# Gated state-space block and expert layer on one core: dt*u*B of two pairs by ScalarE's scaling and TensorE's transpose

## What is computed

```python
def step(state, xs):
    d_t, B_t, C_t, u_t = xs
    dA = jnp.exp(d_t[..., None] * A)
    state = state * dA + (d_t * u_t)[..., None] * B_t[:, None, :]
    y_t = jnp.einsum('ben,bn->be', state, C_t)
    return (state, y_t)
...
y = y + D[None, :, None] * u
y = y * jax.nn.silu(z)
```

## Time and profile before

| what | value |
|---|---|
| three runs | 563.35, 566.0 and 566.44 us; median 566.0 us |
| profiled execution | 564.01 us, of which the span is 562.3 us |
| mean granted clock of PE | 0.975 |
| PE busy | 503.3 us (90%), weight loads 379.6 us |
| POOL busy | 481.5 us (86%) |
| DVE busy | 459.7 us (82%) |
| ACT busy | 395.1 us (70%) |
| HBM | 66 GB/s over the span |

### The profile page before, as it was taken

The page is one execution under the profiler, slowest core; times in us unless marked ns, Lnnn a source line. Parts: engine busy times, 40 slices in busy tenths (PEclk is TensorE's granted clock), DMA queues, the critical chain, the costliest instruction groups (busy, mean ns, idle before and its releaser), DMA issues.

```text
span 562.3 us, 9366 instructions
## 1 busy us (share of the span) xinstructions
PE 503.3 (90%) x3146; PEld 379.6 (68%) x3146; DVE 459.7 (82%) x842; ACT 395.1 (70%) x702; POOL 481.5 (86%) x361
## 2 busy tenths in 40 slices
PE   6577988988789999999999999999999998999496
PEld 2156977868576878579786967686676676567452
DVE  2798999969899989688999989696877788787640
ACT  3468688577958686577958685688877886796321
POOL 0179999999999999989999999799999999888600
PEclk9978999999999999999999999999999999999869
DMA  5792000146120001063300000363000000000000
GB/s 113 289 354 89 2 2 1 38 134 208 75 76 2 1 0 57 27 256 136 106 8 19 2 20 2 142 213 138 1 20 19 20 2 19 20 21 0 20 0 37
DMA packets 18130, 37.82 MB, mean 67 GB/s; under 512 B 5521, under 2 KB 6033, under 8 KB 18082
## 3 DMA queue, kind: packets, MB, share of 16 engines
q1 hardware_dynamic: 18082, 37.22, 19.2%
HBM read 32.75 MB, written 4.46 MB: 66 GB/s over the span
## 4 chain that ended last, share of the span: by engine, by line
PE 52%; ACT 14%; POOL 13%; DVE 11%; issue 8%; DMA 1%; DVEq 0%; ACTq 0%; SPq 0%; POOLq 0%
PE p_s L700 14%; PE p_y L719 11%; POOL state L523 8%; PE p_v L751 6%; PE p_f L742 5%; DVE state L1144 4%; PE p_tr L666 4%; POOL dbu L510 3%; ACT da L923 3%; PE p_pr L629 2%; DVE x L1092 2%; ACT p_s L923 2%; PE p_pr L622 2%; ACT L875 2%; PE p_pr L641 2%
## 5 line engine op out<-in xcount | busy, mean ns | idle before, releaser
L523 POOL TENSOR_TENSOR state<-state,c_bc 128x1024 f32<-128x1024 f32 (+1 forms) x160 | 306.5, 1929 | 15.4 <-DVE state L1144 12.5
L1144 DVE TENSOR_TENSOR_SCAN state<-da,p_s 128x512 f32<-128x512 f32 (+1 forms) x158 | 172.7, 1103 | 27.9 <-PE p_s L700 26.2
L700 PEld LDWEIGHTS p_s<-pair_b,du_t 128*128 128x128 f32 x1264 | 162.3, 195 | 36.5 <-issue 23.5
L700 PE MATMUL p_s<-pair_b,du_t 128*128 128x128 f32 x1264 | 177.0, 280 | 4.3 <-DVE state L1144 3.2
L719 PE MATMUL p_y<-ident,state 128*128 128x128 f32 x1024 | 149.6, 274 | 1.2 <-POOL state L523 1.2
L923 ACT ACTIVATE da<-delta,a_neg 128x512 f32<-128x512 f32 (+1 forms) x190 | 119.2, 642 | 25.2 <-DVE state L1144 24.7
L719 PEld LDWEIGHTS p_y<-ident,state 128*128 128x128 f32 x1024 | 119.5, 141 | 21.8 <-issue 16.3
L510 POOL TENSOR_TENSOR dbu<-du,pair_b 128x1024 f32<-128x1024 f32 (+1 forms) x64 | 116.5, 1820 | 2.9 <-DMA pair_b<-bc_rows 2.9
L1144 DVE TENSOR_TENSOR_SCAN state<-p_s,dbu 128x512 f32<-128x512 f32 (+1 forms) x98 | 101.1, 1037 | 5.5 <-POOL dbu L510 4.4
L923 ACT ACTIVATE p_s<-delta,a_neg 128x512 f32<-128x512 f32 (+1 forms) x130 | 74.9, 581 | 38.6 <-DVE state L1144 37.9
L742 PE MATMUL p_f<-u_sb,h_t 128*128 128x512 f32 x112 | 55.2, 595 | 1.5 <-DVE gw L1236 1.5
(11 more groups left out here) (172 smaller groups left out, 616.4 us busy)
## 6 DMA issues: line engine op xcount, KB each, us to landing
c_bc<-bc_rows SPq DMA_DIRECT2D x32, 512.0 KB, 5.5
pair_b<-bc_rows SPq DMA_DIRECT2D x13, 512.0 KB, 5.6
xs<-in_x SPq DMA_DIRECT2D x16, 256.0 KB, 4.5
out<-ot SPq DMA_DIRECT2D x14, 256.0 KB, 2.0
cx<-in_ctx_t SPq DMA_DIRECT2D x4, 512.0 KB, 3.7
u_sb<-in_u_w SPq DMA_DIRECT2D x1, 1024.0 KB, 6.8
v_sb<-in_v_w SPq DMA_DIRECT2D x1, 1024.0 KB, 14.7
out<-state SPq DMA_DIRECT2D x2, 256.0 KB, 2.0
```

The source lines that it names most:

```text
L523: eng.tensor_tensor(pair, pair, c_bc[:, 2 * p:2 * p + 2, c0:c0 + w], ALU.mult).then_inc(po_cs, 1)
L700: mm = eng.matmul(p_s[g % BANKS][:, t * P:(t + 1) * P], du_t[:, f % 2, t, :], diagonals_of(n // 2)[:, n % 2, c0 // P + t, :], start=(t == ...
L1144: eng.tensor_tensor_scan(slot(g)[:, 0:w], decayed, added, first, ALU.mult, ALU.add).then_inc(ve_scan, 1)
```

## The change

In phases 3, 7 and 11 the tiles of the last two PE pairs (pairs 6 and 7 in phase 3, pairs 5 and 7 in phases 7 and 11) are made in another way. ACT scales each of the 4 blocks of `du_t` by the column of `b_t`, one instruction for each block, and writes the result over the diagonal of the same block in `pair_b`, which is not needed again. PE then only transposes the block, with the identity as the moving operand. It makes 12 tiles, 48 blocks, in this way. ACT's four scalings of a tile stand behind `decay` of n = 0, 2, 4 and 6 and wait for the copy of du and for PE's last use of the diagonal, in the phase before. `make_dbu` of such a tile waits for the last of its four scalings. `copy_b` waits for all scalings of the earlier batches, since it writes `b_t`.

```diff
+    def by_scale(f, p):
+        b, k = PHASE[f][:2]
+        return k == Q - 1 and b + 1 < B and p in pe_pairs(b)[-2:]
+
+    SCALED = [(f, n, t) for f in range(F) for n in range(NS) if by_scale(f, n // 2) for t in range(Q)]
...
-                if b == 0 and n == 0:
+                scaled = by_scale(f, n // 2)
+                if scaled:
+                    eng.wait_ge(ac_scale, SCALED.index((f, n, Q - 1)) + 1)
+                elif b == 0 and n == 0:
...
                 for t in range(w // P):
-                    mm = eng.matmul(p_s[g % BANKS][:, t * P:(t + 1) * P], du_t[:, f % 2, t, :], diagonals_of(n // 2)[:, n % 2, c0 // P + t, :],
-                                    start=(t == 0), stop=(t == w // P - 1))
+                    to = p_s[g % BANKS][:, t * P:(t + 1) * P]
+                    by_b = diagonals_of(n // 2)[:, n % 2, c0 // P + t, :]
+                    if scaled:
+                        mm = eng.matmul(to, by_b, ident[:, :], is_transpose=True, start=(t == 0), stop=(t == w // P - 1))
+                    else:
+                        mm = eng.matmul(to, du_t[:, f % 2, t, :], by_b, start=(t == 0), stop=(t == w // P - 1))
...
                     if b > 1:
                         eng.wait_ge(ac_diag, 2 * Q * (b - 1))
+                    eng.wait_ge(ac_scale, sum(PHASE[f][0] < b for f, n, t in SCALED))
...
+            def scale_du(f, n):
+                eng.wait_ge(ac_turn, TURN["du", f] + 1)
+                eng.wait_ge(pe_dbu, by_pe[f - 1, n] + 1)
+                for t in range(Q):
+                    eng.activation(diagonals_of(n // 2)[:, n % 2, t, :], du_t[:, f % 2, t, :], ACT.Copy,
+                                   scale=b_t[:, n, t:t + 1]).then_inc(ac_scale, 1)
...
                     decay(f, n)
+                    if turning and n in (0, 2, 4, 6):
+                        scale_du(f, 2 * pe_pairs(b)[-2:][n // 4] + n // 2 % 2)
```

More of the change, by code:

```diff
@@ L244, in flamingo @@
         ac_da = sem("act_decay")
+        ac_scale = sem("act_du_times_b")
         ac_diag = sem("act_diagonals")
```

## The result

| | before | after |
|---|---|---|
| median of 20 runs, us | 565.77 (563.35 to 567.96) | 569.74 (566.41 to 574.81) |
| profiled execution, us | 564.01 | 569.51 |
| its span, us | 562.3 | 567.5 |
| mean granted clock in it | 0.975 | 0.966 |

The ratio is 1.0085 with a 95% interval of 1.0066 to 1.0103: slower, by 4.8 us (3.7 to 5.8). The two medians of the table are 4.0 us apart; the text goes by the recorded ratio and its interval. The forecast was +0.55%, 569.1 us; the sign and the range held, the size was too small. The interval of the difference leaves the forecast's 3.1 us out.

What follows compares the result with a forecast made beforehand. POOL's full, fixed-order stretches were taken as the bound. Phase 3's 1.4, phase 7's 0.5 and phase 11's 1.2 us sum to +3.1 us on the 566.0 us median: 569.1 us, +0.55%, range 564.5 to 571.5 us.

Steps and rivals of the forecast that it cites:

- What bounds the kernel: POOL's full stretches (131.4 to 237.3, 251.1 to 354.7, 364.7 to 469.0 us): one started late ends as late.
- PE's part: Phases 3, 7 and 11: twelve changed tiles save 5.3 us of PE; only up to 0.3 us counts, in phase 7.
- ACT's price: 48 added scalings hold ACT's queue 0.295 us each, 1.2 us a tile; upper bound 0.39 each, 1.6 a tile.
- Phase 3: Third and fourth groups make ACT 2.4 us late; 1.01 us idle before decay 9 gives back: +1.4 us.
- Phase 7: Exp of the scores 2.0 us later, PE 0.8; POOL's idle time before pairs 3 and 5 absorbs most: +0.5 us.
- Phase 11: POOL's pair 2 starts 2.0 us later; pair 3 had 0.82 us of idle time: +1.2 us.
- The clock: Rival: transposes lower PE's granted clock to the ends of changed phases, 9 us on top, 578 us; chance 0.03.

Runs made afterwards that it cites:

- experiment 1: Kernel before plus ACT's 48 scalings at the change's places, written into a buffer nobody reads; PE makes all tiles by products: 571.46 us, ratio 1.0095.
- the first of 8: Kernel before with only the small copy moved up right behind the copy of silu(z), first of two measurements: 562.58 us, ratio 0.9938.
- experiment 2: Changed kernel without the scalings; PE transposes the twelve tiles, which hold other values: 565.22 us, ratio 0.9996 to the kernel before.
- experiment 4: Changed kernel with its four scaling groups behind decays 0, 1, 2 and 4, so only the third keeps its late place: 571.60 us, ratio 1.0117.
- experiment 5: Changed kernel with its four scaling groups behind decays 0, 1, 2 and 6, so only the fourth keeps its late place: 564.32 us, ratio 0.9981.
- experiment 6: Changed kernel with the small copy moved right behind the copy of silu(z), ahead of the third scaling group: 566.22 us, ratio 1.0012.
- experiment 7: Changed kernel with PE's dt projection moved behind the work of n = 5 in the changed phases: 567.61 us, ratio 1.0039.
- experiment 3: Changed kernel with all four scaling groups early, behind decays 0, 1, 2 and 3: 565.00 us, ratio 0.9997.
- 9 (the second kernel): Changed kernel, groups behind decays 0 to 3, small copy behind silu(z) copy, dt projection behind n = 5 work in changed phases: 564.38 us, ratio 0.9977.

## Why the prediction was right, and where not

**What bounds the kernel: right.** The first full stretch is 100.03 us before and after, and within 0.07 us of it in ten of the twelve runs of experiments. In the two others (experiment 1 and the first of 8) it is 1.0 us longer, with a granted clock of 0.93 from 130 to 180 us where the others have 0.97, so a lower clock may get past PE's lead there. Otherwise what starts the stretches late ends them late.

**PE's part: right.** A turned tile takes 0.44 us of PE's queue. PE's timeline in phase 3 of the kernel after:

```profile
132.84 0.60 PE L715 MATMUL p_s<-ident,pair_b 128*128 128x128 f32 x4
133.28 1.04 PE L735 MATMUL p_y<-ident,state 128*128 128x128 f32 x8
```

Twelve such tiles save 5.4 us (the forecast had 5.3 for twelve times 0.45), and they are worth nothing that the runs can tell (experiment 2); by the steps phase 7 gives 0.4 us against a forecast of up to 0.3. One small gain I didn't have: the second stretch is 0.28 to 0.30 us shorter with the turned tiles.

**ACT's price: right.** Four scalings hold the queue 1.17 us; the forecast was 1.2. The estimate of 0.41 us each by the Trainium skill ("ScalarE: Activation LUTs", Rules for kernel authors), which I had set against the pitch of 0.295 us, would have made 1.6; the rows bear out the pitch.

**Phase 3: right in size, half wrong in its way.** I took 1.4 us: ACT 2.4 us late, less 1.01 of idle time. It is 1.17, with and without the fourth group (experiment 4), and nothing with the fourth alone (experiment 5). I had PE's delay of the scan of tile 6 too, but not that decay 9 waits for this very scan: the third group's 1.17 us reach softplus that way in full, and what the idle time hides is the fourth group. ACT's own way, the one that I summed, is there too and about as long (1.13 us, experiment 6). So it is partly luck that 1.4 came so near.

**Phase 7: right.** +0.5 was forecast, +0.32 is there; PE's wait grew by 0.73 for a forecast of 0.8. Exp of the scores starts 1.91 us later against S than before (6.24 us in place of 4.33), for a forecast of 2.0. It reaches POOL as forecast, pair 2 waiting 2.42 us in place of 0.51, and most of it is absorbed before pair 5. The third group alone gives the same step, 19.99 (experiment 4), so here too PE's way is as long.

**Phase 11: the step that was mis-sized.** I forecast +1.2. Without the fall of the clock it is +0.89 (experiments 6 and 7: 19.26 against 18.37), near enough. With it the step is +2.41. Experiments 6 and 7 take PE's wait away together with the fall, and no execution has this wait in phase 11 without a fall. But in phase 7 of experiment 4 the same wait without a fall makes pair 3 only 0.74 us late against S, and in phase 11 of experiment 6 exp alone makes it 1.04 us late, so the wait by itself should add nothing. So the delays add up to 1.17 + 0.32 + 0.89 = 2.4 us where I had 3.1, and the term that I put at nothing is the fall, 1.5 us in this execution. The sum fell short by that term.

**The clock: right that the turned tiles don't lower it, wrong to stop there.** The rule that I cited from the Trainium skill ("TensorE: Matmul & The Clock Gate", Part 4: PE-mode transpose), that the full clock doesn't engage for transposes, is not borne out here either: with twelve turned tiles and no late copy the granted clock around them stays at 1.00 (experiments 2 and 3). But I looked for a fall by what PE would do and not by what PE would wait for. In the 14 profiled executions, three places each, PE waits 1.50 to 1.94 us for the small copy in 10 (the kernel after, experiments 1 and 4, phase 3 of experiment 7), and in 5 of these the granted clock of the 10 us around the copy is 0.66 or 0.83: phase 11 three times of three, phase 7 once of three, phase 3 once of four. In the other 32, where PE waits 0.88 us or not at all, it is 1.00 each time. A fall costs 1.5 us in phase 11 (20.78 against 19.26), 2.2 in phase 3 (experiment 1 against the kernel after) and some 1.7 in phase 7 (the 2.11 between the same two, less the 0.41 that the turned tiles give there, experiment 2; ahead of these tiles pair 3 starts 14.69 us behind S in experiment 1 and 13.00 in the kernel after). By the steps without a fall, 3.5 - 1.5 = 2.0 us, the measured 4.8 us would be one or two falls in a mean execution, as an estimate. The runs' mean clocks agree: of the 20 runs of the kernel after, the 8 below 0.965 took 571.6 to 574.8 us and the 12 others 566.4 to 571.4; the kernel before, with a mean clock below 0.965 in 14 of the 90 runs beside the experiments, took at most 568.4 in them.

**What stays open.** That the wait brings the fall is argued from where the falls lie, and from their absence where the wait was taken away (experiment 6, and phases 7 and 11 of experiment 7), in one profiled execution of each kernel. It isn't shown by a wait of this length put in by itself, and why 5 of 10 such waits pass without a fall isn't settled. Low mean clocks have a second source, which no wait for the copy explains: the first 30 us, with a granted clock of 0.82 or 0.83 in the executions of experiments 5, 7, 8 (the first) and 9 (the second kernel), whose mean clocks are 0.957 to 0.967 without a fall at a copy. What sets it there was not tried; since it comes ahead of all that is changed, it may spread the times of every kernel here, and why experiment 7 measured +2.2 us where its steps give +1.0 may lie there, which isn't shown.

## What to carry to other kernels

Find the queue that has a fixed order and no gaps, and read which wait starts it; time saved elsewhere, 5.4 us of PE here, is worth what it moves that start. Work added to an engine that looks idle costs by its place. The same four scalings cost nothing ahead of an instruction for which ACT had to wait anyway. Behind that instruction they cost over a microsecond, because a copy came next for which PE was already waiting. Where an engine has such a short wait, ask whether what it waits for can move up: moving one call ahead of its neighbours gained 2.6 us here (3.5 in the first measurement).

## What was unexpected of the hardware

A wait of PE of 1.5 to 1.9 us, between stretches of dense work, can be followed by TensorE's 1.2 GHz level for some microseconds: the two dt products behind it took 1.90 us in place of 1.12, and p_v's four 3.00 in place of 1.96. It followed 5 of 10 such waits here and none of the 32 shorter ones or places without one; that the wait is its cause was not tested by itself. So the price of a late copy may be not only its delay but as much again. Also, two paths that were each made about 1.2 us longer gave 1.2 us together, and the same with either of them left (experiments 4 and 6): single waits of a trace say what ends last, not what stands right behind.
